# The next batch's scores moved ahead of the value products in a two-layer attention kernel

## The chip, the cores and the metric

The kernel runs on one core of one Trainium2 chip, as one program. The metric is the device time of that core in microseconds: 718.37 us before, the median of 3 runs (717.77 to 719.16).

## The reference

```
x = x + cross_attention_0(layernorm(x), ctx)     # 16 heads of 64, rope, mask, softmax
x = x + int4_linear_plus_lora(layernorm(x))      # 128 -> 128
x = x + cross_attention_1(layernorm(x), ctx)     # 16 heads of 8, mask, softmax
x = x + bitlinear_gated_ffn(layernorm(x))        # 128 -> 512 -> 128
```

x has 32 batches of 128 rows of 128 features, ctx has 77 rows of 128 features for each batch. The change is in `cross_attention_1`, "the second attention":

```
q = Q @ Wq_w + Wq_b ; k = K @ Wk_w + Wk_b ; v = V @ Wv_w + Wv_b      # 16 heads of 8
scores = einsum('bhqd,bhkd->bhqk', q, k) / sqrt(8), masked
out = softmax(scores) @ v
return out @ Wo_w + Wo_b
```

## The kernel before

The whole x stays in SBUF, and four stages follow each other: the first attention, the int4 layer (its products run inside the second attention's loop), the second attention and the last feed-forward stage. Every engine runs an order written out by hand, and waits on semaphores.

The second attention works in slots, one for each batch b. Two batches make a pair p; j is 0 for the first batch of a pair ("even slot") and 1 for the second ("odd slot"). `pairs_loop` writes out pairs 0 to 3, loops over pairs 4 to 13 two at a time (so a body has four slots, with P = p mod 2), and writes out pairs 14 and 15.

For one batch the work runs as a chain over the engines:

1. TensorE, `score_maxima(b)`: the scores in bf16 with the rows of x down the partitions. First the mask is written by products with an identity (L1912 with 128 rows of weights, L1916 with four tiles of 64 x 64), then four products over 64 features each (L1921 to L1929). The features are split in halves that lie in different rows of the array, and the last product waits on `half_done` until L1921 has ended.
2. VectorE, `maxima(b)`: three reductions of the banks (L1674 twice, L1677) and a maximum of the two results (L1678, `maxima_ready`).
3. TensorE, `turn_maxima(b)` (L1935): turns the maxima. ScalarE, `fold_in(b)` (L1806): copies them beside the mask.
4. TensorE, `scores(b)` (L1942): ten fp32 products over 64 rows of weights each, two passes each, in pairs on the two halves of the array, with the keys down the partitions. `folds(b)` (L1960): ten bf16 products that add mask and maxima to them.
5. ScalarE, `exps(b)` (L1812). TensorE, `values(b)` (L1975, L1981): twenty fp32 products over 128 rows into 64 columns each.
6. VectorE, `normalise(b)` (L1683, L1684). TensorE, `turn_out(b)` (L1989), ScalarE `turned_out(b)` (L1817), TensorE `out_projection(b)` (L1993), VectorE `residual(b)` (L1689).

Steps 6 of batch b run in slot b + 1, and step 1 and 2 of batch b + 1 run in slot b. Beside this chain a slot has work for later pairs. In the even slot TensorE turns the rows of the next pair (`transposes`, L1884), makes its queries and keys (`queries_keys`, L1893), and turns the rows of the int4 layer of pair p + 2 (`ffn_turn`, L1999) and later multiplies them (`ffn_project`, L2006). In the odd slot it makes the values (`values_rows`, L1901). In every fourth slot it turns four batches for the last stage (L395).

VectorE's queue in a slot begins with `normalise(b - 1)`. In an even slot, `start.statistics(p + 2)` (L218 to L224) comes next, then work for the last stage (L338 and L372 to L374, or L362), and then `start.rows(p + 2)` (L236), which waits for the power that GpSimd takes of the variance (L228). `residual(b - 1)`, `maxima(b + 1)` and `queries(p + 1)` follow. `ffn_turn(p + 2)` waits for `start.rows(p + 2)`, through `start.xhat_ready`.

Of the kernel before, what the change touches and what calls it, by code (L numbers as in the profile page):

```python
# [1434 lines left out]
def layer1_attention(nc, ctx, t):  # L1435
# [39 lines left out]
    m_full, fold_ready, maxima_ready, half_done = sem("m_full"), sem("fold_ready"), sem("maxima_ready"), sem("half_done")  # L1475
    vals_ready = sem("vals_ready")
# [162 lines left out]
    def vector(dve, third):  # L1639
# [31 lines left out]
        def maxima(b):  # L1671
            for i in (1, 0):
# [3 lines left out]
            dve.wait_ge(x_full[2], b + 1)  # L1676
            steps.link(nc.vector.tensor_reduce(max_r[:], pr[:, 0:256].rearrange("p (h k) -> p h k", k=RPAD), AX, ALU.max))  # L1677
            nc.vector.tensor_tensor(row_max, max_m[:], max_r[:], ALU.max).then_inc(maxima_ready, 1)  # L1678
# [88 lines left out]
        pairs_loop(dve, slot, steps, 56)  # L1767
# [110 lines left out]
    def tensor(pe, third):  # L1878
# [27 lines left out]
        def score_maxima(b, p, P, j, first):  # L1906
            pe.wait_ge(maxima_ready, b)
            if not first:
                out_projection(b - 2)

# [26 lines left out]
        def scores(b, P, j):  # L1937
# [7 lines left out]
            score(2, 0, 0, 4, True).then_inc(half_done, 1)  # L1945
# [3 lines left out]

            pe.wait_ge(half_done, 2 * b + 2)  # L1950
            score(2, 1, 1, 4, False)
            score(0, 3, 0, 3, False)
            score(1, 3, 1, 3, False)
# [80 lines left out]
        score_maxima(0, 0, 0, 0, True)  # L2034
        yield
        turn_maxima(0)

        def slot(b, p, P, j, more, g, prev):
# [3 lines left out]
            scores(b, P, j)  # L2042
# [3 lines left out]
            if j == 0:  # L2046
                score_maxima(b + 1, p, P, 1, first)
            elif more:
                score_maxima(b + 1, p + 1, 1 - P, 0, False)
            else:  # L2050
                out_projection(b - 1)
            if pair(p, 1) and j == 0:
                pe.wait_ge(front.means_read, 1)
            if j == 0 and more_pre(p):
                ffn_turn(p + 2)
            if j == 0 and more:
                queries_keys(p + 1)
            if j == 1 and more:
                values_rows(p + 1)
            if pair(p, PAIRS - 1) and j == 0:  # L2060
# [9 lines left out]
            if back(P, j, prev):  # L2070
                pe.wait_ge(f_done, p + 3 if more_pre(p) else PAIRS)
                front.rows(pe, prev, pm)
            if j == 0 and more_pre(p):
                ffn_project(p + 2)
            if j == 0 or more:
                turn_maxima(b + 1)
# [339 lines left out]
```

## Time and profile before

| | |
|---|---|
| median of 3 runs | 718.37 us |
| the profiled execution | 719.26 us |
| its span | 716.7 us |
| TensorE (PE) busy | 680.4 us, 95% |
| VectorE (DVE) busy | 556.9 us, 78% |
| GpSimd (POOL) busy | 432.1 us, 60% |
| ScalarE (ACT) busy | 388.7 us, 54% |
| mean granted clock of TensorE | 0.995 of full speed |

PE is the products, PEld the loads of their weights. A matmul's duration runs to the modelled end of its way through the array, so products that follow each other overlap: the time that one costs is the distance from its start to the start of the next, and "100% busy" doesn't say that the array works at its peak. In a row of the timeline, "x20" says that 20 instructions are merged.

### The profile page before, as it was taken

What the parts mean: (1) busy time and instruction counts of PE and PEld (TensorE: products, weight loads), DVE (VectorE), ACT (ScalarE), POOL (GpSimd) and SP (SyncE); (2) the same over time, 40 slices, a digit from 0 to 9 for tenths busy, and PEclk for the clock granted to TensorE, in tenths of its full rate; (3) what the DMA queues carried; (4) which work ended last, traced back from release to release, by engine and by line L of the source; (5) the groups of instructions that cost most, each with busy time, mean ns of one, the idle gap of its engine ahead of it and who ended that gap; (6) DMA issues with size and microseconds to landing.
All of it is one profiled execution on the core that took longest, in us unless ns stands there. A gap on an engine that the chain in (4) does not pass through costs nothing.

```text
span 716.7 us, 23519 instructions
## 1 busy us (share of the span) xinstructions
PE 680.4 (95%) x9268; PEld 569.8 (80%) x9273; DVE 556.9 (78%) x1635; ACT 388.7 (54%) x846; POOL 432.1 (60%) x558
## 2 busy tenths in 40 slices
PE   8999999999999999999999989999999999998875
PEld 6788888888888888889888878788888888875544
DVE  5887787697687698688687655787878887778996
ACT  2443553543544544445345444566766766766896
POOL 3597586487396388378477523455555646632775
PEclk9999999999999999999999999999999999998999
DMA  9511011101101101101100120000000000000011
GB/s 263 132 34 37 13 48 45 33 5 46 37 26 45 36 2 45 36 26 36 36 22 15 32 79 7 11 7 7 12 5 4 9 4 9 0 2 1 24 45 52
DMA packets 26766, 23.82 MB, mean 33 GB/s; under 512 B 7148, under 2 KB 23356, under 8 KB 26680
## 3 DMA queue, kind: packets, MB, share of 16 engines
q1 hardware_dynamic: 25864, 22.25, 11.1%
q8 instruction: 62, 1.02, 0.6%
q10 hardware_dynamic: 816, 0.36, 0.2%
q14 instruction: 24, 0.20, 0.1%
HBM read 10.25 MB, written 2.10 MB: 17 GB/s over the span
## 4 chain that ended last, share of the span: by engine, by line
PE 70%; DVE 17%; POOL 5%; issue 4%; ACT 3%; DMA 1%; SPq 0%; ACTq 0%; DVEq 0%
PE bank L1274 7%; PE bank L1316 6%; PE bank L1942 6%; PE bank L1172 5%; PE bank L1296 4%; PE bank L1975 4%; PE bank L1278 4%; PE bank L1307 3%; PE bank L1173 3%; PE bank L1174 3%; DVE a_am L911 3%; PE bank L1960 2%; DVE f_h_max L2192 2%; PE bank L1223 2%; PE bank L1232 2%
## 5 line engine op out<-in xcount | busy, mean ns | idle before, releaser
L741 POOL TENSOR_TENSOR a_turned<-a_turned,a_rope 128x512 f32<-128x512 f32 x63 | 81.7, 1297 | 55.7 <-DVE a_turned L848 55.7
L742 POOL TENSOR_TENSOR a_qr<-a_straight,a_turned 128x512 f32<-128x512 f32 x64 | 81.6, 1276 | 4.9
L845 DVE TENSOR_TENSOR a_straight<-bank,a_rope 128x512 f32<-128x512 f32 x63 | 43.0, 683 | 52.5 <-PE bank L1174 51.4
L1045 ACT CAST a_qb<-a_qr 128x512 bf16<-128x512 f32 x64 | 39.8, 622 | 65.9 <-POOL a_qr L742 65.9
L1296 PE MATMUL bank<-a_vs,a_probs 77*64 77x65 f32 x2048 | 66.8, 222 | 0.0
L1296 PEld LDWEIGHTS bank<-a_vs,a_probs 77*64 77x64 f32 x2048 | 62.6, 137 | 3.3
L753 POOL TENSOR_TENSOR a_k_turned<-a_k_turned,a_rope 128x308 f32<-128x308 f32 x61 | 48.4, 793 | 24.3 <-DVE a_k_turned L858 23.6
L1316 PE MATMUL bank<-a_wo,a_oTn 128*128 128x128 f32 x512 | 62.6, 275 | 0.2 <-ACT a_oTn L1073 0.2
L1316 PEld LDWEIGHTS bank<-a_wo,a_oTn 128*128 128x128 f32 x512 | 60.5, 192 | 1.2 <-ACT a_oTn L1073 0.5
L911 DVE TENSOR_REDUCE a_am<-bank 128x6 bf16<-128x462 f32 (+1 forms) x96 | 49.9, 576 | 12.1 <-PE bank L1232 12.0
L1274 PE MATMUL bank<-a_qr,a_kr 64*77 64x128 f32 x960 | 59.2, 273 | 0.0
L1057 ACT COPY a_fold<-bank 112x128 bf16<-112x128 bf16 x32 | 8.5, 266 | 92.4 <-PE bank L1244 92.4
L1067 ACT ACTIVATE a_probs<-bank 77x512 f32<-77x512 f32 x98 | 52.8, 593 | 7.5 <-PE bank L1258 7.5
L1274 PEld LDWEIGHTS bank<-a_qr,a_kr 64*77 64x77 f32 x960 | 52.3, 144 | 5.2 <-issue 5.1
L755 POOL TENSOR_TENSOR a_kr<-a_k_straight,a_k_turned 128x308 f32<-128x308 f32 x62 | 52.0, 840 | 4.8
L848 DVE STREAM_SHUFFLE a_turned<-bank 128x512 f32<-128x512 f32 x63 | 46.3, 735 | 0.0
L1674 DVE TENSOR_REDUCE a_max_m<-bank 128x8 f32<-128x512 f32 x64 | 41.1, 685 | 5.0 <-PE bank L1923 4.6
L1812 ACT ACTIVATE a_qr<-bank 128x512 f32<-128x512 f32 (+1 forms) x96 | 43.8, 536 | 1.0 <-PE bank L1960 1.0
L729 POOL TENSOR_TENSOR a_rstd<-a_var,minus_half 128x2 f32<-128x2 f32 x16 | 11.3, 707 | 51.1 <-DVE a_var L812 51.0
L1073 ACT COPY a_oTn<-bank 128x512 f32<-128x512 f32 x64 | 34.5, 589 | 13.4 <-PE bank L1307 12.8
L1172 PE MATMUL bank<-a_xT_hi,a_wq_hi 128*128 128x256 f32 x128 | 39.9, 312 | 1.3 <-DVE a_wq_lo L939 1.1
L1599 POOL TENSOR_TENSOR a_kr<-a_k_straight,a_blocks 128x128 f32<-128x128 f32 x32 | 12.8, 400 | 46.4 <-ACT a_k_straight L1794 46.4
(282 smaller groups left out, 1984.8 us busy)
## 6 DMA issues: line engine op xcount, KB each, us to landing
a_vs<-a_stage SPq DMA_DIRECT2D x16, 312.8 KB
out<-x_all SPq DMA_DIRECT2D x16, 128.0 KB, 1.8
x_all<-in_x_dram SPq DMA_DIRECT2D x7, 256.0 KB, 6.3
a_vs<-a_stage SPq DMA_DIRECT2D x4, 308.8 KB
a_mask_in<-in_mask SPq DMA_DIRECT2D x16, 77.0 KB, 5.7
a_wv<-in_ctx SPq DMA_DIRECT2D x16, 77.0 KB
a_ctx_in<-in_ctx SPq DMA_DIRECT2D x8, 128.0 KB
a_vs<-a_stage SPq DMA_DIRECT2D x4, 211.2 KB
```

The source lines that it names most:

```text
L741: steps.link(nc.gpsimd.tensor_tensor(tv, tv, rope[:, 1:2, :].broadcast_to([128, 4, S]), ALU.mult))
L742: nc.gpsimd.tensor_tensor(qr[P][:, 2 * k:2 * k + 2, :, :].rearrange("p t j s -> p (t j) s"), sv, tv, ALU.subtract if made else ALU.add).th ...
L753: steps.link(nc.gpsimd.tensor_tensor(tv, tv, rope[:, 3:4, 0:KL].broadcast_to([128, 4, KL]), ALU.mult))
L755: nc.gpsimd.tensor_tensor(kr[q % 2][:, lo:hi, first:end, :].rearrange("p i j s -> p i (j s)"), view(k_straight[n % 3]), view(k_turned[n % ...
L848: nc.vector.stream_shuffle(turned[k % 3][:], pv, mask=[lane ^ 1 for lane in range(32)]).then_inc(a_free[TASK["Q", p, k][0]], 1)
L911: nc.vector.tensor_reduce(rows, ps[bk][:, 0:n * KL].rearrange("p (h k) -> p h k", k=KL), AX, ALU.max).then_inc(s_free[bk], 1)
L1067: nc.scalar.activation(probs[:, 4 * g:4 * g + 4, :], ps[ST_BANK[g]][0:KL, :].rearrange("p (h s) -> p h s", s=S), ACT.Exp).then_inc(s_free[ ...
L1172: nc.tensor.matmul(out, lhs_hi, rhs_hi, start=True, stop=False)
L1274: nc.tensor.matmul(banks[g][0:KL, i * S:(i + 1) * S], kr[b // 4 % 2][e:e + 64, h // 2, b % 4, :], qr[P][e:e + 64, h // 2, j, :], start=i = ...
L1296: last = nc.tensor.matmul(po[r][rows, VW * i:VW * (i + 1)], probs[:, PROBS_SLOT[h], rows], vs[b % RING][:, h, :], start=True, stop=True)
L1316: last = nc.tensor.matmul(po[2][:, 0:D], oTn[:, i, :], wo[:, i, :], start=i == 0, stop=i == TILES - 1)
L1812: nc.scalar.activation(probs[:, 4 * g:4 * g + n, :], SCORES[g].rearrange("p (t s) -> p t s", s=S), ACT.Exp).then_inc(s_free[g], 1)
```

## The change

TensorE's order in a slot changes. `scores(b + 1)` follows directly behind `score_maxima(b + 1)`, ahead of `values(b)`, where `scores(b)` stood at the start of slot b before. `turn_out(b - 1)` and `folds(b)` so follow directly behind `turn_maxima(b)` of the slot before (with `ffn_project` or `transposes` between). `queries_keys`, `ffn_turn` and `values_rows` move ahead of `out_projection(b - 1)` and `score_maxima(b + 1)`. VectorE reduces the small bank `pr` first, signals `rest_read`, and the score products into that bank wait for it; inside `scores` the order is changed so that these come late.

```
--- before.py
+++ after.py
@@ -1473,6 +1473,7 @@
         sem(n) for n in ("turned_in", "ctx_repeated", "q_ready", "k_ready", "vals_in"))
     x_full, s_full, s_free = ([sem(f"{n}{i}") for i in range(3)] for n in ("x_full", "s_full", "s_free"))
     m_full, fold_ready, maxima_ready, half_done = sem("m_full"), sem("fold_ready"), sem("maxima_ready"), sem("half_done")
+    rest_read = sem("rest_read")
     vals_ready = sem("vals_ready")
 
     keys_ready, cast_done = [sem(f"keys_ready{j}") for j in range(2)], [sem(f"cast_done{j}") for j in range(2)]
@@ -1669,12 +1670,15 @@
                                            kept_all[:], ALU.add, ALU.mult).then_inc(q_ready, 1)
 
         def maxima(b):
+            dve.wait_ge(x_full[2], b + 1)
+            nc.vector.tensor_reduce(max_r[:], pr[:, 0:256].rearrange("p (h k) -> p h k", k=RPAD), AX,
+                                    ALU.max).then_inc(rest_read, 1)
             for i in (1, 0):
                 dve.wait_ge(x_full[i], b + 1)
                 steps.did(nc.vector.tensor_reduce(max_m[:, 8 * i:8 * i + 8],
                                                   px[i][:].rearrange("p (h k) -> p h k", k=KM), AX, ALU.max))
-            dve.wait_ge(x_full[2], b + 1)
-            steps.link(nc.vector.tensor_reduce(max_r[:], pr[:, 0:256].rearrange("p (h k) -> p h k", k=RPAD), AX, ALU.max))
+            steps.wait()
+            dve.wait_ge(rest_read, b + 1)
             nc.vector.tensor_tensor(row_max, max_m[:], max_r[:], ALU.max).then_inc(maxima_ready, 1)
 
         def normalise(b):
@@ -1764,7 +1768,7 @@
             if j == 0 and more:
                 queries(p + 1, 1 - P)
 
-        pairs_loop(dve, slot, steps, 56)
+        pairs_loop(dve, slot, steps, 52)
         normalise(B - 1)
         next(third)
         residual(B - 1)
@@ -1903,11 +1907,8 @@
                                         start=True, stop=True)
             last.then_inc(values_full, 1)
 
-        def score_maxima(b, p, P, j, first):
+        def score_maxima(b, p, P, j):
             pe.wait_ge(maxima_ready, b)
-            if not first:
-                out_projection(b - 2)
-
             pe.wait_ge(s_free[2], b)
             nc.tensor.matmul(pr[:, 0:256].rearrange("p (h k) -> p h k", k=RPAD), t["identb"][:],
                              ampad[:, KM:KP].rearrange("p (a k) -> p a k", a=1).broadcast_to([S, H1, RPAD]),
@@ -1942,15 +1943,17 @@
                 return nc.tensor.matmul(SCORES[g][:, i * S:(i + 1) * S], keys[P][FEATURES[half], j, 128 * tile:128 * tile + 128],
                                         q1[P][FEATURES[half], j, :], start=first, stop=False, skip_group_check=True)
 
-            score(2, 0, 0, 4, True).then_inc(half_done, 1)
             for i in range(3):
                 score(1, i, 1, i, i == 0)
                 score(0, i, 0, i, i == 0)
 
+            pe.wait_ge(rest_read, b + 1)
+            score(2, 0, 0, 4, True).then_inc(half_done, 1)
+            score(1, 3, 1, 3, False)
+            score(0, 3, 0, 3, False)
+
             pe.wait_ge(half_done, 2 * b + 2)
             score(2, 1, 1, 4, False)
-            score(0, 3, 0, 3, False)
-            score(1, 3, 1, 3, False)
 
         def folds(b):
             pe.wait_ge(fold_ready, b + 1)
@@ -2031,32 +2034,34 @@
         values_rows(0)
         yield
         pe.wait_ge(setup, 11)
-        score_maxima(0, 0, 0, 0, True)
+        score_maxima(0, 0, 0, 0)
         yield
         turn_maxima(0)
+        scores(0, 0, 0)
 
         def slot(b, p, P, j, more, g, prev):
             first = isinstance(b, int) and b == 0
             if j == 0 and more:
                 transposes(p + 1, 1 - P)
-            scores(b, P, j)
             if not first:
                 turn_out(b - 1)
             folds(b)
-            if j == 0:
-                score_maxima(b + 1, p, P, 1, first)
-            elif more:
-                score_maxima(b + 1, p + 1, 1 - P, 0, False)
-            else:
-                out_projection(b - 1)
             if pair(p, 1) and j == 0:
                 pe.wait_ge(front.means_read, 1)
+            if j == 0 and more:
+                queries_keys(p + 1)
             if j == 0 and more_pre(p):
                 ffn_turn(p + 2)
-            if j == 0 and more:
-                queries_keys(p + 1)
             if j == 1 and more:
                 values_rows(p + 1)
+            if not first:
+                out_projection(b - 1)
+            if j == 0:
+                score_maxima(b + 1, p, P, 1)
+                scores(b + 1, P, 1)
+            elif more:
+                score_maxima(b + 1, p + 1, 1 - P, 0)
+                scores(b + 1, 1 - P, 0)
             if pair(p, PAIRS - 1) and j == 0:
                 pe.wait_ge(front.xqT_ready, PAIRS // 2 - 2)
                 front.turn_weight(pe, 0, pm)
@@ -2070,10 +2075,10 @@
             if back(P, j, prev):
                 pe.wait_ge(f_done, p + 3 if more_pre(p) else PAIRS)
                 front.rows(pe, prev, pm)
+            if j == 0 or more:
+                turn_maxima(b + 1)
             if j == 0 and more_pre(p):
                 ffn_project(p + 2)
-            if j == 0 or more:
-                turn_maxima(b + 1)
 
         pairs_loop(pe, slot)
         next(third)
```

## Rows read from the trace of the kernel before

**Rows 1.** Windows: the loop, then the start of the last stage.

```profile
core 0: us, PE busy (x) PEld busy (x) DVE busy (x) ACT busy (x) POOL busy (x), PEclk, DMA share, GB/s
474.70:604.70 130.00, 130.00 (x1915) 106.77 (x1912) 104.49 (x408) 86.89 (x220) 75.80 (x128) 1.00 0.02 7
...
659.00:667.00 8.00, 7.05 (x33) 4.54 (x34) 7.86 (x22) 4.01 (x6) 4.55 (x7) 0.57 0.00 1
```

**Rows 2.** Source L1935, one in each slot: ns min/median/max, first and last start.

```profile
L1935 PE MATMUL bank<-identb,s_am x32: 219/219/263, 448.6 to 649.7; 128*112 128x128 bf16 x32
```

**Rows 3.** Waits of PE from 445 to 670 us: total, times, longest.

```profile
PE bank L2290 <- DVE a_oTn L2184: 2.2, 2, 1.9
```

**Rows 4.** Timeline, all engines, an even slot: PE from its scores to the values.

```profile
540.14 1.39 PE L1942 MATMUL bank<-a_wq,a_straight 64*128 64x128 f32 x20
...
541.45 0.33 PE L1989 MATMUL bank<-ident,a_wv 128*128 128x128 f32 x1
...
541.62 0.72 PE L1960 MATMUL bank<-a_qr,a_fold_w 112*128 112x128 bf16 x10
...
542.23 0.46 PE L1993 MATMUL bank<-a_wo,a_wv 128*128 128x128 f32 x2
...
542.53 0.27 PE L1912 MATMUL bank<-s_ampad,identb 128*128 128x256 bf16 x1
...
543.07 0.23 PE L1921 MATMUL bank<-a_k_turned 64*128 64x128 bf16 x1
...
543.36 0.23 PE L1929 MATMUL bank<-a_k_turned 64*128 64x128 bf16 x1
...
543.55 0.41 PE L1999 MATMUL bank<-ident,s_xhat 128*128 128x128 f32 x2
...
543.80 0.60 PE L1893 MATMUL bank<-a_wk,a_wq 128*128 128x256 f32 x2
...
544.59 1.11 PE L1975 MATMUL bank<-a_kr,a_qr 128*64 128x18 f32 x32
...
545.54 0.45 PE L1981 MATMUL bank<-a_kr,a_qr 128*64 128x72 f32 x8
545.92 0.71 PE L2006 MATMUL bank<-f_w,a_wv 128*128 128x128 f32 x4
...
546.47 0.22 PE L1935 MATMUL bank<-identb,s_am 128*112 128x128 bf16 x1
```

**Rows 5.** The same timeline: VectorE and ScalarE in that slot.

```profile
539.99 0.29 DVE L1684 TENSOR_TENSOR a_wv<-bank,a_rec 128x128 f32<-128x128 f32 x1
...
541.98 1.37 ACT L1812 ACTIVATE a_qr<-bank 128x256 f32<-128x256 f32 x3
...
542.62 0.60 DVE L236 TENSOR_SCALAR s_xhat<-x_all,s_mv,s_rstd 128x128 f32 x2
...
543.50 1.29 DVE L1674 TENSOR_REDUCE a_max_m<-bank 128x8 f32<-128x512 f32 x2
...
544.71 0.41 DVE L1677 TENSOR_REDUCE a_max_r<-bank 128x16 f32<-128x256 f32 x1
...
546.04 0.26 DVE L1683 RECIPROCAL a_rec<-bank 128x16 f32<-128x16 f32 x1 [0.32 <-PE bank L1981]
...
546.33 0.29 DVE L1684 TENSOR_TENSOR a_wv<-bank,a_rec 128x128 f32<-128x128 f32 x1
...
546.73 0.26 ACT L1806 COPY a_qr<-bank 16x128 bf16<-16x128 bf16 x1 [0.57 <-PE bank L1935]
```

**Rows 6.** The same timeline, the odd slot behind it: products of the values.

```profile
550.00 0.49 PE L1901 MATMUL bank<-a_wv,a_qr 128*128 128x128 f32 x2
...
551.09 1.11 PE L1975 MATMUL bank<-a_kr,a_qr 128*64 128x18 f32 x32
```

**Rows 7.** Timeline, VectorE in the next even slot.

```profile
552.83 0.29 DVE L1684 TENSOR_TENSOR a_wv<-bank,a_rec 128x128 f32<-128x128 f32 x1
...
555.22 0.60 DVE L236 TENSOR_SCALAR s_xhat<-x_all,s_mv,s_rstd 128x128 f32 x2
```

More of the change, by code:

```diff
@@ L1675, in maxima @@
                                                   px[i][:].rearrange("p (h k) -> p h k", k=KM), AX, ALU.max))
-            dve.wait_ge(x_full[2], b + 1)
-            steps.link(nc.vector.tensor_reduce(max_r[:], pr[:, 0:256].rearrange("p (h k) -> p h k", k=RPAD), AX, ALU.max))
+            steps.wait()
+            dve.wait_ge(rest_read, b + 1)
             nc.vector.tensor_tensor(row_max, max_m[:], max_r[:], ALU.max).then_inc(maxima_ready, 1)
@@ L1765, in slot @@
                 queries(p + 1, 1 - P)
-        pairs_loop(dve, slot, steps, 56)
+        pairs_loop(dve, slot, steps, 52)
         normalise(B - 1)
@@ L1904, in values_rows, with score_maxima @@
             last.then_inc(values_full, 1)
-        def score_maxima(b, p, P, j, first):
+        def score_maxima(b, p, P, j):
             pe.wait_ge(maxima_ready, b)
-            if not first:
-                out_projection(b - 2)
             pe.wait_ge(s_free[2], b)
@@ L1948, in scores @@
                 score(0, i, 0, i, i == 0)
+            pe.wait_ge(rest_read, b + 1)
+            score(2, 0, 0, 4, True).then_inc(half_done, 1)
+            score(1, 3, 1, 3, False)
+            score(0, 3, 0, 3, False)
             pe.wait_ge(half_done, 2 * b + 2)
             score(2, 1, 1, 4, False)
-            score(0, 3, 0, 3, False)
-            score(1, 3, 1, 3, False)
         def folds(b):
@@ L2045, in slot @@
             folds(b)
[L2046 to L2051, printed above, removed]
             if pair(p, 1) and j == 0:
                 pe.wait_ge(front.means_read, 1)
+            if j == 0 and more:
+                queries_keys(p + 1)
             if j == 0 and more_pre(p):
                 ffn_turn(p + 2)
-            if j == 0 and more:
-                queries_keys(p + 1)
             if j == 1 and more:
                 values_rows(p + 1)
+            if not first:
+                out_projection(b - 1)
+            if j == 0:
+                score_maxima(b + 1, p, P, 1)
+                scores(b + 1, P, 1)
+            elif more:
+                score_maxima(b + 1, p + 1, 1 - P, 0)
+                scores(b + 1, 1 - P, 0)
             if pair(p, PAIRS - 1) and j == 0:
@@ L2072, in slot @@
                 front.rows(pe, prev, pm)
+            if j == 0 or more:
+                turn_maxima(b + 1)
             if j == 0 and more_pre(p):
                 ffn_project(p + 2)
-            if j == 0 or more:
-                turn_maxima(b + 1)
         pairs_loop(pe, slot)
```

9 lines of the change are left out of this document (6 added, 3 removed).

## The prediction

> **What bounds the kernel now.** I read four views: the windows, the list of waits, the timeline of one even and one odd slot on TensorE, and the timeline of VectorE over the same stretch.
>
> The windows show a second attention in which TensorE counts as busy all the time: 130.00 of 130.00 us at a granted clock of 1.00, while VectorE has 104.49, ScalarE 86.89 and GpSimd 75.80 [rows 1]. The one line that each slot runs once starts at 448.6 for the first time and at 649.7 for the last, 31 slots apart, so a slot takes 201.1 / 31 = 6.49 us and a pair 12.97 [rows 2]. The list of waits tells the same: in 225 us the longest wait of TensorE is of 1.9 us and belongs to the last stage [rows 3]; inside the loop it waits for nobody. So the loop goes by TensorE's own order, and what its starts are apart is what counts.
>
> These distances in the even slot are [rows 4]: scores 1.31 (540.14 to 541.45), `turn_out` 0.17, folds 0.61, `out_projection` 0.30, masks 0.54, maxima products 0.29 to the last of them and 0.19 behind it, `ffn_turn` 0.25, queries and keys 0.79, values 1.33 (1.40 to their end at 545.99), `ffn_project` 0.55. In the odd slot `values_rows` takes 1.09 [rows 6]. What the reader is to see besides: ten folds take 0.06 each, but the product behind the last 128-column maxima product, which is of the same length, comes 0.19 behind it. The 0.13 between is what a change from 64 rows of weights to 128 costs at its first product; single `turn_out` behind such a change takes another 0.05 more than the 0.12 of a turn in `ffn_turn`.
>
> Under this cover lie chains over other engines that today cost nothing. From the end of the values to the end of `normalise` pass 0.63 us (545.99 to 546.62), and the scores of the next slot hide them; `fold_in` ends 0.52 behind the start of the turn of the maxima [rows 4, 5]. And from the end of `normalise` to the end of `start.rows` pass 2.94 us in one even slot (540.28 to 543.22) and 2.70 in the next (553.12 to 555.82) [rows 5, 7]. `ffn_turn` needs the latter; it comes at 543.55, 3.27 behind `normalise`, just late enough [rows 4].
>
> **The switches removed.** Scores behind the maxima products need no change of rows. Three changes go in each slot: into the scores, out of them, and out of the maxima products; the one into the values stays. At 0.13 to 0.19 each (the 0.13 above, and with the 0.05) that is 0.39 to 0.57 us in a slot; I take 0.43, a gain, since a part returns as the step from bf16 to fp32 inside the stretch. For 32 slots that is 14 us, if nothing else happened.
>
> The Trainium skill, in "TensorEngine Tiling (Array Packing)", section Key Properties, says that a change of the tiling mode drains the engine, while tiles of one mode work on beside each other. By this trace the rule agrees: the 0.13 is that drain. By the rule alone the change could only gain; what it leaves out here is who was hidden by the products that moved.
>
> **The wait inside the stretch.** The second score product into `pr` waits for the end of the first one, through `half_done`. Before, the first stood at the very start of the scores and was long done. Now one other pair of products stands between. The same wait among the maxima products costs a distance of 0.29 from start to start [rows 4]; a pair of fp32 products covers 0.26 of such a wait (1.31 / 5), but as a product has two passes and only the last one releases, I take 0.2 left over (bounds 0 and 0.3). `rest_read` itself is hidden: VectorE needs 0.41 for the small bank [rows 5], the products ahead of that wait take three fifths of 1.31.
>
> **VectorE's order.** It reduces the same three banks, 1.29 + 0.41 us [rows 5], and one step of its own counter goes: 0. The large banks now come last, but the turn of the maxima stands behind scores and values, 2.7 us of products: covered. ScalarE's three exponentials take 1.37 [rows 5] and the scores of the next batch wait for them; between folds and scores TensorE has over 2 us of products in either slot: covered.
>
> **Behind the values.** What hid `normalise` is gone. `turn_out` can start 0.63 + 0.06 behind the end of the values (0.06 is the step from one product's end to the start of the product that waits for it, 543.07 + 0.23 to 543.36 [rows 4]). `turn_maxima` and `ffn_project` or `transposes` cover the larger part of it; 0.15 to 0.35 us stay open. Queued behind `turn_out` is all of TensorE's slot.
>
> **The even slot.** This is the step that decides. `ffn_turn` now stands ahead of `out_projection` and of the maxima products. Behind `normalise` TensorE needs only 0.06 + 0.17 + 0.61 + 0.79, less the drain in the last, some 1.55 us, until it gets there. The rows that it turns are ready 2.70 to 2.94 behind `normalise`: VectorE's queue is statistics, GpSimd's power, work for the last stage, then the two products of L236, and none of this can begin before `normalise`, which is first in that queue. I take 2.75, as the 2.94 holds a queue on GpSimd that should be shorter with the values made earlier. So TensorE stands still for 1.2 us. Behind it are `out_projection`, the maxima products and the scores, and VectorE's residual and maxima wait for those.
>
> From the end of `normalise`: 2.75 + 0.06, `ffn_turn` 0.25, `out_projection` 0.30, masks 0.54, 0.29 to the last maxima product: 4.19. From there 0.10 to the scores (no drain), 1.31, 0.2 of waiting, 1.40 of values, 0.63 to the next `normalise`: 3.64. The even slot takes 7.8 us.
>
> The odd slot has no `ffn_turn`: 0.06 + 0.17 + 0.61 + 1.09 + 0.30 + 0.54 + 0.29 = 3.06, less 0.10 for a drain that `values_rows` no longer has in front, and 3.64: 6.6 us. Here VectorE reaches its maxima about when they are ready, since residual and the rows of the second attention lie in front; up to 0.25 in one of two odd slots is in the range, not in the sum.
>
> **The sum.** A pair takes 14.4 instead of 12.97 us. Some starts overlap more than their distances in the old order tell (the 0.30 of `out_projection` holds a step from bf16 to fp32 that now falls to another product), so I take +1.3. `ffn_turn` runs in 14 pairs, the first two without the last stage's work on VectorE, 0.4 less each: 14 x 1.3 - 0.8 = 17.4. The last two pairs have no such wait, their slots take some 6.6 instead of 6.49, but the last slot has no scores: -0.5. The setup is as long as before. The profiled execution of 719.26 becomes 736.2; it lies 0.9 above the median of 718.37, so against that 735 us, +2.3%.
>
> **The rivals.**
>
> *Only `normalise` is exposed.* If `ffn_turn`'s rows are ready when TensorE comes (because TensorE reaches it later than I sum, or the statistics run sooner), the even slot is 6.6 like the odd one, and a pair 13.2: 16 x 0.2 = 3 us more, 721.6; with the bounds 717 to 725. Against it speak two measured even slots with 2.70 and 2.94. 9%.
>
> *Faster, by the switches.* The removed switches rule if both `normalise` and `ffn_turn` stay covered, 0.43 saved less 0.2 of `half_done`: 32 x 0.23 = 7 us, 711. The mechanism is that TensorE's instructions behind the values last longer than VectorE's two steps; the point is 0.69 us behind the values, and 1.55 against 2.7 for `ffn_turn`. This is also what the page's rule would give, 704 (14 us less) by the rule alone. 6%.
>
> *The clock falls.* Today it is at 1.00 in the loop, but in the last stage a wait of 1.9 us stands just ahead of a stretch at 0.57, where most of the time was at the lower of its two levels, 1.2 instead of 2.4 GHz [rows 1, 3]. Should the two idle pieces of each even slot do the same, part of the loop runs at half speed: a tenth of the 200 us is 20 us more, 755. The idle pieces here are shorter and dense work lies between. 5%.
>
> *As I forecast:* 80%, by itself 727 to 742: the bounds are 0.3 and 0 for the `half_done` wait (32 x 0.2 = 6 us down, 3 up), 2.65 to 2.94 for the rows (2 us either way), 0.25 for late maxima in each second odd slot (2 us up).
>
> The range for 8 in 10 is 723 to 742. Of the rival that exposes only `normalise` a third falls within 0.2% (1.4 us, about what a measurement of this kernel can tell from no change) or below. Faster 0.07, same 0.04, slower 0.89.
>
> **What the next profile would show.** TensorE's waits would name L236 ahead of L1999, 14 times, some 1.2 us each, and L1684 ahead of L1989, about 0.2 each. L1942 would start 0.1 behind L1929, with its last two passes some 0.2 late. The distance of L1935 from slot to slot would be near 7.8 and 6.6, and TensorE's busy share in the loop would fall to some 90%. I would be wrong if L1999 followed L1893 without a gap, or if the gap stood there and the slot were still no longer than before, because then the products would have cost less than their distances told.

## The result

| | before | after |
|---|---|---|
| median | 718.76 us (4 runs) | 739.67 us (4 runs) |
| ratio | | 1.0292 (95% interval 1.0266 to 1.0318) |
| profiled execution, its span | 719.26, 716.7 | 741.27, 738.7 |
| PE, DVE, ACT, POOL busy | 680.4, 556.9, 388.7, 432.1 | 690.0, 566.5, 383.9, 431.9 |

The kernel is 20.9 us slower. The forecast was 735 us, slower, with a range of 723 to 742. All times here and below are of executions in the fast state; one execution of "statistics only" (1073.52 us, at a mean granted clock of 0.55) was in the slow one and is not counted.

First the instructions of the turn of the maxima, one in each slot (its line is L1936 now), for the same reading as in [rows 2]; then the windows, for that of [rows 1]:

```profile
L1936 PE MATMUL bank<-identb,s_am x32: 219/263/264, 449.3 to 672.6; 128*112 128x128 bf16 x32
```

```profile
474.00:604.00 130.00, 122.06 (x1721) 100.68 (x1721) 101.06 (x367) 75.27 (x198) 66.92 (x112) 1.00 0.02 7
464.00:467.00 3.00, 1.55 (x19) 1.33 (x19) 2.08 (x11) 2.26 (x7) 0.69 (x1) 1.00 0.11 32
467.00:470.00 3.00, 2.61 (x13) 1.80 (x13) 1.26 (x5) 0.98 (x4) 1.65 (x3) 0.67 0.00 0
```

From the first to the last turn pass 223.3 us, where it was 201.1 [rows 2]: 22.2 more. The span grew by 22.0, so all of it is in this loop. In 130 us of it TensorE is busy 122.06, against all of them before [rows 1].

The waits of TensorE, over 445 to 680 us (total, times, longest). Inside the loop the kernel before had a few short ones beside the line in [rows 3], 2.0 us together; the longest of them was

```profile
PE bank L1884 <- DVE a_wq L1660: 0.7, 1, 0.7
```

and the changed kernel has:

```profile
PE bank L2002 <- DVE s_xhat L236: 6.4, 8, 1.0
PE bank L1963 <- ACT a_qr L1810: 3.9, 6, 0.7
PE bank L1897 <- DVE f_w_mean L305: 1.8, 1, 1.8
PE bank L1992 <- DVE a_wv L1688: 1.2, 3, 0.5
```

L2002 is `ffn_turn`, and its wait leads the list. The view of L236 names, beside these 8, another 12 in which the weight load of L2002 is what waited (9.5 us in all); how such a wait is shared between the two records varies, so the distances of the starts say more. This is the timeline of TensorE over an odd slot and the even one behind it (compare [rows 4, 6]):

```profile
546.16 0.33 PE L1992 MATMUL bank<-ident,a_wv 128*128 128x128 f32 x1
546.32 0.72 PE L1963 MATMUL bank<-a_qr,a_fold_w 112*128 112x128 bf16 x10
546.88 0.44 PE L1905 MATMUL bank<-a_wv,a_qr 128*128 128x128 f32 x2
...
548.88 0.23 PE L1930 MATMUL bank<-a_k_turned 64*128 64x128 bf16 x1
548.98 1.71 PE L1943 MATMUL bank<-a_wq,a_straight 64*128 64x128 f32 x20
550.62 1.11 PE L1978 MATMUL bank<-a_kr,a_qr 128*64 128x18 f32 x32
551.57 0.45 PE L1984 MATMUL bank<-a_kr,a_qr 128*64 128x72 f32 x8
551.95 0.26 PE L1936 MATMUL bank<-identb,s_am 128*112 128x128 bf16 x1
...
552.27 0.30 PE L1890 MATMUL bank<-ident,a_wv 77*128 77x77 f32 x2
552.71 0.33 PE L1992 MATMUL bank<-ident,a_wv 128*128 128x128 f32 x1
...
553.92 0.42 PE L1898 MATMUL bank<-a_k_straight,a_wk 128*128 128x154 f32 x2
555.13 0.44 PE L2002 MATMUL bank<-ident,s_xhat 128*128 128x128 f32 x2 [0.79 <-DVE s_xhat L236]
...
556.46 0.23 PE L1930 MATMUL bank<-a_k_turned 64*128 64x128 bf16 x1
...
559.52 0.26 PE L1936 MATMUL bank<-identb,s_am 128*112 128x128 bf16 x1
```

And VectorE over the even slot (compare [rows 5, 7]):

```profile
552.36 0.29 DVE L1688 TENSOR_TENSOR a_wv<-bank,a_rec 128x128 f32<-128x128 f32 x1
...
553.45 1.12 DVE L362 TENSOR_SCALAR a_vs<-x_all,f_mv,f_rstd 128x128 f32 x4
554.48 0.60 DVE L236 TENSOR_SCALAR s_xhat<-x_all,s_mv,s_rstd 128x128 f32 x2
```

What to see: `normalise` ends at 552.65, TensorE is through queries and keys some 1.5 us later and stands still until the rows of L236, ready at 555.08. The product that waited for them starts at 555.13. In the odd slot, scores to values are 1.64 apart (548.98 to 550.62) where the scores took 1.31.

The times between two turns of the maxima, from the starts of that line in the trace of each kernel, are these for the four slots of a loop body (even P = 0, odd, even P = 1, odd with the turn of four batches):

```
                               even0  odd0  even1  odd1   sum
before                          6.78  5.88   6.89  6.44  25.99
after                           7.37  6.55   7.57  7.04  28.53
ffn_turn behind the maxima      7.28  6.55   6.79  7.07  27.69
statistics first                7.06  6.55   6.57  7.07  27.25
folds first                     7.36  6.48   7.57  6.94  28.35
three together                  7.03  6.58   6.56  6.90  27.07
all covers                      7.19  6.48   6.42  6.51  26.60
four batches earlier            6.52  6.48   6.48  6.87  26.35
statistics first, small bank last   7.29  6.77   6.80  7.27  28.13
statistics first, bank earlier      7.03  6.52   6.54  7.07  27.16
statistics only                     7.06  6.55   6.69  7.04  27.34
scores alone                        7.44  7.57   7.58  7.99  30.58
before, statistics first            6.78  5.88   8.04  6.48  27.18
before, work moved                  7.84  6.44   7.09  6.39  27.76
```

One slot stands out: the even slot of pair 1 takes 9.68 instead of 6.83. There the first pair's odd slot has turned the sums of the last stage's weights into the bank that `ffn_turn` uses, and the code waits for VectorE's reduction of them ahead of `queries_keys`, as it stood behind the maxima products before. That is the wait of 1.8 for L305, and behind it come 3 us at a granted clock of 0.67 (467 to 470, in the windows above), which is a mixture of the two levels of 1.2 and 2.4 GHz; in the 3 us ahead TensorE was busy for 1.55. With the same wait of 1.84 us, but with the clock at 1.00 behind it, the slot takes 8.48 in the next kernel below. So of the 2.85 some 1.65 are the wait, and some 1.2 the lower clock.

### The profile page after: what moved, and what is told of

Same layout as the page of the kernel before. It is cut to its first block, busy times and chain, and to the rows that moved or that the text cites. A ratio compares the mean times of both kernels' runs of the same rounds, so it can differ in the third digit from the quotient of the medians.

```text
span 738.7 us, 23567 instructions
## 1 busy us (share of the span) xinstructions
PE 690.0 (93%) x9268; PEld 579.2 (78%) x9273; DVE 566.5 (77%) x1635; ACT 383.9 (52%) x846; POOL 431.9 (58%) x558
## 3 DMA queue, kind: packets, MB, share of 16 engines
q8 instruction: 62, 1.02, 0.6%
## 4 chain that ended last, share of the span: by engine, by line
PE 69%; DVE 20%; issue 5%; ACT 3%; POOL 2%; DVEq 0%; ACTq 0%; POOLq 0%
PE bank L1943 7%; PE bank L1274 7%; PE bank L1316 6%; PE bank L1172 5%; PE bank L1296 4%; PE bank L1978 4%; PE bank L1173 4%; PE bank L1278 4%; PE bank L1174 4%; PE bank L1307 3%; DVE a_am L911 3%; PE bank L1321 2%; PE bank L1223 2%; DVE f_h_max L2197 2%; PE bank L1232 2%
## 5 line engine op out<-in xcount | busy, mean ns | idle before, releaser
L228 POOL TENSOR_TENSOR s_rstd<-s_var,minus_half 128x2 f32<-128x2 f32 x16 | 11.4, 710 | 48.9 <-DVE s_var L224 48.9
```

## The experiments

Each edit is on the changed kernel where nothing else is said. The kernels were timed in sets, and the kernel before in each of them: 718.76 us beside the changed kernel, 719.87 beside the first four below (`ffn_turn` behind, statistics first, folds first, three together), 718.86 beside small bank earlier, all covers and the two edits of the kernel before, 719.01 beside the other four. A difference between kernels of two sets is uncertain by about the 1 us by which these differ; the ratios are each against the kernel before of the same set.

**ffn_turn behind the maxima products.**

```
                 score_maxima(b + 1, p, P, 1)
+                if more_pre(p):
+                    ffn_turn(p + 2)
                 scores(b + 1, P, 1)
```

(and the call ahead of `out_projection` is taken out)

> ffn_turn goes back behind the maxima products, between them and the scores; all else as in the changed kernel. Theory (the wait for the rows of L236 decides the even slot): the wait ahead of ffn_turn, 0.8 to 1.0 us in the profile of the changed kernel, is gone, since the maxima products take its place and are needed by VectorE; two changes of the array's rows come back, 0.3 us. Even slots go from 7.47 to about 6.9 us, 14 of them: 8 us less than the changed kernel, about 731. Rival (the order behind the values decides, and ffn_turn only absorbs a wait that would stand elsewhere): within 2 us of the changed kernel, 738 to 741. Rival (the stretch of 64-row products is where the time goes): no slot shorter, time up by the two switches, 744.

Measured 733.45, ratio 1.0189 (1.0167 to 1.0211): 6.2 less than the changed kernel, or 7.4 by the two ratios. L236 is gone from the list of waits. The even slot with P = 1 went from 7.57 to 6.79, that with P = 0 only from 7.37 to 7.28: there something else holds TensorE by then, `fold_in`, which stands in ScalarE's queue behind the copy of the four batches. The mechanism holds, and the size is 0.6 to 1.8 us short of 8. In the two profiles 1.2 of the difference are the slot of pair 1, where the clock didn't fall this time; that was not in the theory.

**Statistics first.**

```
+            if j == 0 and more_pre(p):
+                start.statistics(steps, p + 2)
             if not first:
                 normalise(b - 1)
             if j == 0 and more_pre(p):
-                start.statistics(steps, p + 2)
+                start.rows(dve, steps, p + 2)
```

(and `start.rows` is gone from behind the last stage's work)

> TensorE's order stays that of the changed kernel; on VectorE, start.statistics goes ahead of normalise in the even slot and start.rows directly behind it, ahead of the work for the last stage. Theory: the chain normalise, statistics, GpSimd's power, rows is cut to normalise and rows, 0.6 us behind normalise against the 1.5 at which TensorE comes, so the wait at L2002 goes to 0 and even slots take about 6.6 to 6.8 us (of the 7.47): 14 x 0.8 = 11 us less, about 728. Rival (VectorE is the bound in the even slot by its 6.1 us of work): statistics delay normalise by as much as they save, and less than 4 us come back, 736 or more.

Measured 727.96, ratio 1.0116 (1.0099 to 1.0134): 11.7 less, about the 11 of the theory. TensorE's order was not touched, so the chains over VectorE were worth more than half of the 20.9. The slots of this kernel show where: even slots with P = 1 went from 7.57 to 6.57, more than the 0.8 of the theory; those with P = 0 only from 7.37 to 7.06, since `fold_in` holds TensorE there; and the slot of pair 1 takes 6.64 instead of 9.68, since the weight means are no longer late. That slot, 3.0 us with its lower clock, was not in the theory, so that the total came out so near is in part luck. This kernel keeps 1.6 us of waits for `normalise` and 2.6 for `fold_in`:

```profile
PE bank L1963 <- ACT a_qr L1810: 2.6, 6, 0.6
...
PE bank L1992 <- DVE a_wv L1688: 1.6, 3, 0.6
...
PE bank L1897 <- DVE f_w_mean L305: 0.2, 1, 0.2
```

**Folds first.**

```
-            if not first:
-                turn_out(b - 1)
             folds(b)
+            if not first:
+                turn_out(b - 1)
```

> folds(b) ahead of turn_out(b - 1) at the start of a slot; all else as in the changed kernel. Theory (normalise exposed behind the values costs TensorE 0.15 to 0.35 us in a slot, but in the even slots the wait for the rows of L236 hides it): only the 16 odd slots gain, 0.15 each, 2 to 3 us less, about 737; the wait at L2002 grows by what turn_out no longer waits. Rival (the whole queue behind turn_out decides in both kinds of slot): 32 x 0.25 = 8 us less, 732. Rival (the folds wait as long for the turned maxima): same, 740.

Measured 739.64, ratio 1.027 (1.0249 to 1.0291): no change against 739.67, or 1.6 us less by the ratios, with intervals that overlap. The odd slots of the loop body gained 0.07 to 0.10, less than the 0.15 expected, for the folds wait for `fold_in` nearly as long as `turn_out` did for `normalise`; the even ones gained nothing, and the wait at L2002 grew to 7.7 us in total. So in the body the exposed `normalise` by itself costs little: behind the values two chains end within a tenth of each other. The total can't tell more, since two slots outside the body moved it by more than that: in the profiles the slot of pair 1 takes 8.28 instead of 9.68, and the even slot of the last pair 9.84 instead of 6.53. There the folds waited for `fold_in`, and the clock was at its lower level behind it:

```profile
663.42 1.08 PE L1963 MATMUL bank<-a_qr,a_fold_w 112*128 112x128 bf16 x10 [1.01 <-ACT a_qr L1810]
```

```profile
664.00:668.00 4.00, 3.65 (x25) 2.29 (x25) 1.64 (x5) 1.53 (x4) 0.00 (x0) 0.50 0.00 0
```

**Three together.** Statistics first, folds first, the products into the small bank one pair earlier, the wait for the weight means behind `queries_keys`.

> Statistics first, folds first, the score product into the small bank one pair earlier (so that its partner waits less for half_done), and the wait for the last stage's weight means only ahead of ffn_turn. Theory: with both chains covered, what is left are the three switches removed (0.43 us in a slot) less what half_done still costs (0.1): the loop's slots fall to about 6.3 us, and the kernel gets below the one before: 711 to 716. Rival (VectorE becomes the bound, since its even slot holds over 6 us of work and its maxima start late in the odd one): 718 to 725. Rival (the switches were worth less than 0.2 each slot): 718 to 722 with TensorE never waiting.

Measured 726.21, ratio 1.009 (1.0073 to 1.0108). The theory's 711 to 716 failed by 10 us. Over 445 to 650 us the list of TensorE's waits has one line for the products; the list for the weight loads (445 to 665 us) has a second one that matters, the small bank:

```profile
PE bank L1965 <- ACT a_qr L1810: 5.0, 10, 0.8
```

```profile
PEld bank L1943 <- DVE a_max_r L1674: 2.9, 12, 0.3
```

The folds wait for ScalarE's copy of the turned maxima, and some score blocks for VectorE's reduction of the small bank. I had counted the removed switches as a gain of 0.43 a slot, and had not counted these waits.

**The small bank one pair earlier,** alone, on the kernel with statistics first:

```
-            for i in range(3):
+            for i in range(2):
 ...
             pe.wait_ge(rest_read, b + 1)
             score(2, 0, 0, 4, True).then_inc(half_done, 1)
+            score(1, 2, 1, 2, False)
+            score(0, 2, 0, 2, False)
```

> The kernel with statistics first, plus only the other order inside the scores: the first product into the small bank goes one pair earlier, behind the same wait for rest_read. Theory: VectorE's reduction of the small bank ends 0.75 us behind the last maxima product, so the earlier product waits for it where the later one did not, and the wait for half_done becomes shorter by as much as is lost, or less: the scores take 1.77 instead of 1.63, 32 x 0.14 = 4 us more than the 728.0 of that kernel, 732. Rival (half_done is the dearer wait, and its distance counts): 3 us less, 725.

Measured 727.14, ratio 1.0113 (1.0097 to 1.013), against 727.96 and 1.0116: neither the 4 more nor the 3 less. Three of the four slots of the body are 0.03 shorter, the fourth is the same. The 1.77 that I had read in the kernel of three together came with folds first, where VectorE reaches the small bank late. What is won at `half_done` is lost at `rest_read`: the weight loads of L1943 wait for the small bank 9 times, 2.0 us, where they did so once, 0.3 us, in the kernel with statistics first.

**The small bank last,** on the kernel with statistics first:

```
-            pe.wait_ge(rest_read, b + 1)
-            score(2, 0, 0, 4, True).then_inc(half_done, 1)
             score(1, 3, 1, 3, False)
             score(0, 3, 0, 3, False)
+            pe.wait_ge(rest_read, b + 1)
+            score(2, 0, 0, 4, True).then_inc(half_done, 1)
```

> Statistics first, and inside the scores both products into the small bank come last, with no other pair between them: the distance that covers half_done is taken away. Theory (half_done holds TensorE as long as the first of the two takes, less what stands between): 0.1 to 0.2 more in each of 32 slots, the scores' block 1.75 to 1.85 instead of 1.63: 3 to 7 us above the 728.0 of statistics first, 731 to 735. Rival (the drain ahead of the values hides that wait, whatever its length): 728.

Measured 734.91, ratio 1.0225 (1.0208 to 1.0242): 7.0 more than 727.96, or 0.22 for each of 32 slots, and the timeline shows the same 0.21 in one block, 1.85 from the scores to the values:

```profile
550.35 1.93 PE L1943 MATMUL bank<-a_wq,a_straight 64*128 64x128 f32 x20
552.20 1.11 PE L1978 MATMUL bank<-a_kr,a_qr 128*64 128x18 f32 x32
```

The rival, that the drain ahead of the values hides the wait, is out: the distance that was taken from `half_done` is paid in every slot (0.20 to 0.23). This is what the wait grew by, and not what it cost already in the changed kernel, which is read below from a block of scores.

**All covers.** Statistics first, folds first, the weight means' wait moved, and on top the turn of the maxima ahead of that of the four batches, with `fold_in(b + 1)` at the end of ScalarE's slot, ahead of `rows_in`.

> Like the run with three together, but with the score order of the changed kernel, the turn of the maxima ahead of the turn of four batches for the last stage, and fold_in ahead of ScalarE's copy of those four. Theory (each exposed chain is a term of its own): 0.14 less in each slot for the scores (1.77 went to them, against 1.63), 4 us, and up to 0.5 in each of six odd slots, 3 us: 719, level with the kernel before. The removed switches are then paid out, and eaten by half_done and the wait for the turned maxima. Rival (VectorE bounds the loop by now): no better than 724.

Measured 723.42, ratio 1.0059 (1.0042 to 1.0075): 4.4 above the 719 of the theory, just below the rival's 724. The odd slot with the four batches fell from 6.90 to 6.51, but the even slot behind it rose to 7.19: ScalarE's copies for the next pair's queries now stand behind the copy of the four batches, and TensorE waits for those:

```profile
531.53 0.70 PE L1899 MATMUL bank<-a_wk,a_wq 128*128 128x256 f32 x2 [0.32 <-ACT a_k_straight L1780]
```

**Four batches earlier.** As above with `fold_in` back in its place, and

```
             if j == 1 and more:
                 values_rows(p + 1)
+            if back(P, j, prev):
+                pe.wait_ge(f_done, p + 3 if more_pre(p) else PAIRS)
+                front.rows(pe, prev, pm)
```

> Statistics first, folds first, the wait for the weight means only ahead of ffn_turn, fold_in where the changed kernel has it, and the turn of four batches for the last stage right behind values_rows, so that ScalarE has copied them long before the maxima are turned. Theory: neither fold_in nor the next pair's transposed copies stand behind that copy; odd slots with the four batches 6.9 to 7.0, even slots behind them 6.4 instead of 7.2: 26.3 us for four slots, 720 to 722, still above the kernel before, since half_done's 0.2 and what the folds wait for the turned maxima are 0.3 of the 0.43 that the switches gave. Rival (VectorE and GpSimd bound it): 724 or more. Rival (the removed switches are worth more than I took): below 717.

The four slots of the body take 26.35, as expected (26.3). The kernel takes 728.18 (725.05 to 733.07), ratio 1.0125 (1.0068 to 1.0182), and not 720 to 722. The two executions with a mean granted clock of 0.995 and 0.997 took 725.61 and 725.05, the other two, with 0.986 and 0.981, took 730.76 (the profiled one) and 733.07. The loss is in one place outside the body: the last group of four batches is rounded by ScalarE in the same slot in which its turn now comes early,

```profile
645.91 0.63 PE L395 MATMUL bank<-ident,a_vs 128*128 128x128 f32 x4 [2.81 <-ACT a_vs L387]
```

and the stretch from 645 to 662 us then ran at a mean granted clock of 0.60. Those two slots take 12.17 and 9.68 us. A cheap order in the body is thus worth little if one exceptional slot stalls for 3 us.

**Statistics only.** As statistics first, but `start.rows` left behind the last stage's work.

> The changed kernel with only start.statistics ahead of normalise; start.rows stays behind the work for the last stage. In the kernels with rows first, the four products of L362 took 1.95 us while GpSimd worked, against 1.12 in the old place. Theory (rows are needed 1.5 us behind normalise, and would come at 1.8 to 2.1): up to 0.4 of the wait stays in each even slot of the loop, but L362 runs undisturbed: 728 to 732. Rival (the slow L362 was on the path in the kernel with rows first): 725 or below.

Measured 729.26, ratio 1.0137 (1.0117 to 1.0158): 1.3 above statistics first, inside the theory's range. The even slots with P = 1 are 6.69 where they were 6.57; those with P = 0 are the same, 7.06.

**The kernel before with statistics first** (the same edit of VectorE's order on the old kernel).

> The kernel before, with only VectorE's order changed: statistics ahead of normalise, rows directly behind it. Theory: in the old order the rows are ready in time (2.7 to 2.9 us behind normalise against 3.3), so nothing waits for them and the time is that of the kernel before within 1 us. Rival (VectorE's order is a gain by itself, so that the 12 us it gave in the new order say nothing of the exposed wait): 5 us or more below it, 714.

Measured 725.06, ratio 1.0086 (1.0069 to 1.0102): 6.2 slower. Both the theory (no change) and the rival (a gain) fell. The even slot with P = 1 goes from 6.89 to 8.04, the others stay. This is VectorE and GpSimd in that slot:

```profile
543.57 0.61 DVE L236 TENSOR_SCALAR s_xhat<-x_all,s_mv,s_rstd 128x128 f32 x2 [1.52 <-POOL s_rstd L228]
544.09 1.95 DVE L362 TENSOR_SCALAR a_vs<-x_all,f_mv,f_rstd 128x128 f32 x4
...
544.44 0.83 POOL L248 TENSOR_TENSOR x_all<-x_all,f_bias 128x256 f32 x1 [0.91 <-DVE s_xhat L236]
545.23 0.73 POOL L1588 TENSOR_TENSOR x_all<-x_all,a_bo 128x256 f32 x1
```

In the old order GpSimd spreads the values late and so takes the power late; VectorE, which used to do L362 in the meantime, now waits 1.52 for it, does L362 afterwards and in 1.95 instead of 1.12, and comes late to the residual and to the maxima. That costs TensorE twice in this slot. Its value products, which wait for the residual (it ends at 546.24), start 0.44 later behind the keys than before. And it waits 0.55 for the maxima, whose last step beside GpSimd takes 1.08 us where it took 0.17:

```profile
547.80 1.08 DVE L1678 TENSOR_TENSOR s_am<-a_max_m,a_max_r 128x16 bf16<-128x16 f32 x1
...
548.94 0.26 PE L1935 MATMUL bank<-identb,s_am 128*112 128x128 bf16 x1 [0.55 <-DVE s_am L1678]
```

So the edit that gave 11.7 in the new order costs 6 in the old one. This shows that the 11.7 is no general gain of that order on VectorE; it pays where the rows are waited for.

**The kernel before with the work moved.** `queries_keys`, `ffn_turn` and `values_rows` ahead of the maxima products, scores in their old place.

> The kernel before, with the second half of the change alone: queries_keys, ffn_turn and values_rows ahead of out_projection and the maxima products; the scores stay at the start of the slot. Theory: TensorE comes to ffn_turn 1.3 + 0.2 + 0.6 + 0.8 = 2.9 us behind normalise, when the rows are just ready (2.7 to 2.9), so at most 0.1 is lost in an even slot: 719 to 722. Rival (the moved work itself is what costs, since VectorE's maxima then start late, with out_projection and residual late too): 728 or more.

Measured 730.54, ratio 1.0167 (1.015 to 1.0184): the rival's number, and the theory's 719 to 722 failed. `ffn_turn` does come in time. But with that work gone from behind the maxima products only the values are left to cover VectorE's three reductions and their maximum, and TensorE waits for these:

```profile
PE bank L1935 <- DVE s_am L1678: 8.3, 16, 0.9
```

The work that moved was the cover of the maxima. In the changed kernel the scores have taken this part over, which is why that wait is not in its list.

**The scores alone.** The changed kernel with the three pieces of work behind the scores, ahead of the values.

> The changed kernel with queries_keys, ffn_turn and values_rows back behind the maxima products, and now behind the scores too: the stretch of 64-row products comes directly behind folds and out_projection. Theory: ffn_turn comes 3.3 us or more behind normalise and waits for nobody; but the scores must wait for ScalarE's three exponentials, which end some 2.2 us behind normalise in either slot against the 2.0 at which TensorE comes: 0.2 in each slot. Even slots 7.0, odd 6.85: 14 us more than before, 733; the maxima have more cover, so no wait for L1682. Rival (only the wait at ffn_turn matters): 728 as with statistics first. Rival (the exponentials matter more, for turned_out stands ahead of them): over 737.

Measured 752.97, ratio 1.0476 (1.0458 to 1.0493), 20 us beyond the theory, and over the 737 of the second rival, though the exponentials it named are waited for only once (0.5 us). The body's slots take 7.4 to 8.0. In an odd slot the block of scores takes 2.05 from its start to the next product, since VectorE, which has residual and the second attention's rows in front, starts on the small bank at 550.99, 0.72 behind the start of the last maxima product (550.27), and `rest_read` comes late:

```profile
550.38 2.12 PE L1943 MATMUL bank<-a_wq,a_straight 64*128 64x128 f32 x20
552.43 0.49 PE L1905 MATMUL bank<-a_wv,a_qr 128*128 128x128 f32 x2
```

The list of waits names L1943 for the small bank 12 times, 3.0 us, up to 0.8, and its weight loads another 22 times, 8.2 us. This odd slot is 1.02 longer than that of the changed kernel (7.57 against 6.55), and its starts tell how that divides: 0.41 in the block of scores, 0.31 between folds and `out_projection`, which now comes before ScalarE has copied the turned rows, and 0.29 in `out_projection` (0.38 instead of 0.22) and `values_rows` (1.08 instead of 0.95).

```profile
PEld bank L1996 <- ACT a_wv L1821: 6.0, 25, 0.3
```

## Why the prediction was right

**The wait at `ffn_turn`,** the step that was to decide, did: it was put at 1.2 us (rows at 2.75 + 0.06 behind `normalise`, TensorE there at 1.55). Measured in the slot shown: product at 555.13 - 552.65 = 2.48, TensorE there at about 1.53 (553.92 + 0.26 - 552.65). So 0.95; the rows were 0.3 earlier than I took, because L362 no longer waited for GpSimd, which had spread the values early. Statistics first and `ffn_turn` behind the maxima both remove it, and give 11.7 and 6.2 us, of which 3.0 and 1.2 are the slot of pair 1. Over the loop TensorE is busy 94% of the time, where I had written some 90.

**The slot sums.** Forecast 7.8 for the even and 6.6 for the odd slot, 14.4 for a pair and 1.3 more than before after overlaps. Measured 7.37 and 7.57, 6.55 and 7.04: 14.27 for a pair, 1.27 more. The stretch from the last maxima product to the end of the next `normalise` was forecast at 3.64 and is 3.77 (556.46 to 560.23). That the pair came out so near is in part luck, for errors of opposite sign meet in it: the even slots are 0.2 to 0.4 below the forecast, the plain odd one is as forecast, and the odd one with the turn of four batches is 0.45 above it, because that turn (0.56 between the two odd slots of before) was only in the average before and not in my sum of the new one. The 0.13 by which the stretch above is longer than forecast are `half_done`.

**`half_done`:** forecast 0.2 a slot (0 to 0.3), measured 0.32. This is a term of the sum that was mis-sized: 0.12 in each of 32 slots are 3.8 us. The end of one block of scores in the changed kernel shows it, in three views of its last passes, each begun at a later one:

```profile
550.10 0.48 PE L1943 MATMUL bank<-a_wq,a_straight 64*128 64x128 f32 x2
...
550.20 0.49 PE L1943 MATMUL bank<-a_wq,a_straight 64*128 64x128 f32 x2
...
550.41 0.27 PE L1943 MATMUL bank<-a_wq,a_straight 64*128 64x128 f32 x1
```

The last pass that waits for nothing starts at 550.10; the two passes of the product that waits for `half_done` start at 550.20 and 550.41, and the values 0.20 behind the second. In the kernel before the next product also starts 0.20 behind the last pass (547.73 to 547.94). So without the wait the block would end 0.32 earlier, which is the difference between 1.64 and 1.31 to within 0.01. The waiting product pays twice: it starts late, and its second pass comes 0.21 behind the first, where in the block of the kernel before each half of the array starts a pass every 0.11 (ten on each half, 546.62 to 547.73). The run with the small bank last, which takes one more pair out of the distance, adds 0.22 to it.

**The switches:** forecast 0.43 a slot, 14 us, and measured 0.31. The plain odd slot holds the same products before and after, but `ffn_project` lies at its start now. In the new one, `turn_out` stands 0.76 behind the turn of the maxima (545.40 to 546.16), of which 0.66 is `ffn_project` and the wait for `normalise`; less that, it takes 6.55 - 0.66 = 5.89, against 5.88 in the old order. So the removed switches are worth what `half_done` costs, and nothing is left over, where I had 0.23. The starts in the two slots (533.70 to 539.59 in the trace of before, 545.40 to 551.95 in that of the changed kernel) show the 0.31: 0.05 less behind the turn of the maxima (0.15 to 0.10), 0.06 behind the last maxima product (0.16 to 0.10), 0.14 in `values_rows` (1.09 to 0.95) and 0.06 in `out_projection` (0.28 to 0.22). The sum was not hit by this, since it was made from distances and not from the 0.43, but the expectation for three together (711 to 716) was made from it and failed.

**`fold_in`.** I named it as covered by 0.52 behind its turn and then left it out of the sum. In the changed kernel it is the second wait (3.9 us), above all where ScalarE copies four batches ahead of it, and with the other chains covered it is the first (5.0 us). `normalise` alone was worth 0.07 to 0.10 in the odd slots and nothing in the even ones (folds first), where I had left 0.15 to 0.35 open in every slot. Nor is it quite so that TensorE waited for nobody in the loop before: the short waits named with the result were there.

**Outside the body.** In the profiled execution the slot of pair 1 costs 2.8 us more than before, and neither its wait for the weight means nor the lower clock behind it was in the sum. The sum came to 736.2 for that execution, which took 741.27; 2.8 of the 5.1 are this slot. Of the rest, the 3.8 us of `half_done` are about made up for by the shorter wait at `ffn_turn` (14 times 0.25, 3.5 us, an estimate from the one slot shown). What is left was not taken apart.

**The rivals.** Only `normalise` exposed (721.6): `ffn_turn` did wait. Faster by the switches (711): with all covers tried, the best kernel here takes 723.4, and the best loop body (26.35 against 25.99) is still longer than the old one. The clock: in the body it stays at 1.00 with idle pieces of 0.8 to 1.0 us in the even slots; in the loop of this profile it fell only behind the 1.84 us of the slot of pair 1.

What stays open: an order that has the stretch and every cover, in the exceptional slots too, was not found. The best body measured here is 0.36 above the old one for four slots, so over 32 slots it would come out some 3 us above the old kernel (an estimate from these two), not below.

## What to carry to other kernels

Before moving a block on a busy engine, list what it hides at its old place and what it would hide at the new one: here the scores hid `normalise` and `fold_in`, and the work behind the maxima products hid VectorE's reductions. Count the chain that starts at the end of the exposed step, not only the step: 0.63 us of `normalise` cost a tenth at most, the 2.4 behind it cost 0.95 us in each even slot like the one shown. Look also through the slots that are written out apart: one wait of 1.8 us there, with the lower clock behind it, cost 2.85 us, where the whole loop body of four slots lost 2.54.

## What the runs showed of the hardware that was not expected

**VectorE beside GpSimd.** The four products of L362 take 1.12 us in the changed kernel (above), and 1.95 in the old kernel with statistics first, with GpSimd's two sums of 128x256 beside them. The maximum of two small tensors that both lie in SBUF shows it as well. Its durations (minimum, median, maximum, in ns) are, in the kernel before and in the changed one:

```profile
L1678 DVE TENSOR_TENSOR s_am<-a_max_m,a_max_r x32: 174/176/924, 448.2 to 649.5; 128x16 bf16<-128x16 f32 x32
```

```profile
L1682 DVE TENSOR_TENSOR s_am<-a_max_m,a_max_r x32: 174/434/749, 449.1 to 670.9; 128x16 bf16<-128x16 f32 x32
```

The change has moved GpSimd's spreading of keys under this instruction, so the median went from 176 to 434 ns. It cost nothing there, since scores and values cover it; in the old kernel with statistics first the same instruction took 1.08 us in the slot shown, and TensorE waited 0.55 us for it. By the Trainium skill, "SBUF — State Buffer", section "SBUF: two separate sides", VectorE and GpSimd share one pair of ports that is locked for a whole instruction, and a VectorE operation with two inputs in SBUF, or in a mode that takes both ports, waits for it. The durations agree with that; the two reductions from PSUM behind `maxima` did not change, 1.29 us before [rows 5] and 1.28 after.

**The clock.** In the changed kernel, after 1.84 us without a product, in a stretch of 3 us with 1.55 busy, the granted clock of the next 3 us was 0.67, and the four mask products (L1917) stretched from 0.40 to 0.63 us. But the same wait in the profile of `ffn_turn` behind the maxima left it at 1.00:

```profile
467.55 0.70 PE L1897 MATMUL bank<-a_wk,a_wq 128*128 128x256 f32 x2 [1.84 <-DVE f_w_mean L305]
```

```profile
467.00:470.00 3.00, 2.45 (x19) 1.55 (x19) 1.75 (x7) 0.03 (x1) 1.40 (x2) 1.00 0.02 6
```

And with folds first 1.01 us without a product near the end of the loop stood ahead of 4 us at 0.50, while idle pieces of 0.8 to 1.0 us in the body of the changed kernel left it at 1.00. So in these traces the length of one wait does not tell whether the clock falls.
